# The first group's projections reordered for an early start, and 36 more filler matmuls, in a three-stage decoder layer on one core

## The chip, the cores and the metric

The kernel runs on one core of a Trainium2 chip. The time is the device time of one execution in microseconds; the median of three runs of the kernel before is 1218.7 (1215.97 to 1222.55). The profiled execution took 1217.05, of which 1215.3 lie between its first and its last instruction (the span).

## The reference, cut to what matters

x is 16 sequences of 128 rows of 256 numbers, float32. Three stages follow each other, each on a layer norm of what the one before left:

```python
def mamba(h):                                # x = x + mamba(norm(x))
    hs, gate = split(h @ in_proj.T)          # 512 channels each
    u = silu(conv4(hs) + conv_b)             # 4 taps along the sequence
    dt, B, C = split(u @ x_proj.T)           # 64, 16, 16; each rms-normed
    dt = softplus(dt @ dt_proj.T + dt_b)
    h_t = exp(dt * A) * h_(t-1) + dt * u * B # 512 channels x 16 states
    y = (sum_n h_t * C + u * D) * silu(gate)
    return y @ out_proj.T
def mlstm(q, ctx):                           # x = x + mlstm(norm(x), ctx)
    ...                                      # 4 heads of 64, gated causal scores,
    ...                                      # row norm, a norm for each head
def nodes(x):                                # x = x + norm(nodes(norm(x)))
    for c in range(6):                       # a graph of 6 attention nodes
        q, k, v = (ew * (node[..] @ We[..] + be[..]) for each of the three)
        node[c] = act_w[c] * (softmax(q@Wq (k@Wk).T / sqrt(32)) v@Wv) @ Wo[c] + q
```

## The kernel before, in words

The 16 sequences are worked in 8 groups (NG) of two, so that a tile has 256 columns (T). For a group the kernel has three streams of steps: "a" (the mamba stage's projections, 11 steps), "u" (its state sums, 16 units, each a product on VectorE at L1068, "feed", a recurrence along the sequence at L1075, "scan", a product with C at L1084, "weigh", and four matmuls into the bank MY at L539 that fold the states, "add"), "x" (the mlstm stage) and "f" (the six nodes). Four units make a chunk, whose dt and dt*u (dts, dtus) are spread over the partitions by DMA; the first chunk of the first group goes directly (`first_chunk`), the others by way of DRAM. The ring has three buffers: a feed waits until the add three units before it is done.

The order in which each engine issues the steps is written out: every step has a number (A_AT, U_AT, X_AT, P_AT, W_AT, plus a shift for each group), all steps of all groups are sorted by it into ORDER, and each engine walks that list and issues its part (`walk`). An engine works its instructions in that order and waits with semaphores (`after`). While the nodes of group g run on TensorE, the mamba and mlstm stages of group g+1 run beside them; only the first group has nothing beside it. So there is a start-up of two parts: the head (from the launch to the first feed), and the stretch from the first state sums to the first node.

Into the start-up also falls the preparation of the node weights ("prep", three parts for each of six nodes). TensorE multiplies the edge weights into the query, key and value weights (12 matmuls at L465) and the edge biases by the weights (12 matmuls with one column at L473, four at L453), ScalarE reads the products (L755), VectorE scales the rest (L981, L982) and the biases (L986, L988, L993). SyncE loads the next node's eight weight tiles of 256 KB (L358) once the last part has let the staging tiles go (w_used).

Warm steps ("w", L479) are matmuls of 128x256 on constants into the bank FA, whose product nobody reads: 10 before the walk and 24 in it. The profile counts a float32 matmul as two passes.

The head of the first group, in the order of its chain: LayerNorm of x (VectorE, L1001 to L1009), transposes (TensorE, L484), four products with win in the bank MA, each waiting until ScalarE has read the one before (L506; L774 and L779 read the first two, L785 and L788 the gates), the convolution (VectorE, L1031, six operations for each half of the channels), Silu (L788 to L792), x_proj (L515), the rms norm (L797 to L802, L1040, whose result is xdn), dt_proj (L528), the softplus (L811 to L827, L1046, L1051), and the DMAs of the first chunk.

## Time and profile before

| What | Value |
|---|---|
| median of three runs | 1218.7 us |
| profiled execution | 1217.05 us, span 1215.3 us |
| TensorE busy | 1086.6 us (89% of the span) |
| VectorE busy | 980.1 us (81%) |
| ScalarE busy | 733.2 us (60%) |
| mean granted TensorE clock | 0.95 of full speed |
| DMA | 76.06 MB, 63 GB/s over the span |

Busy times count each engine alone and overlap each other. The clock is the one that the chip granted TensorE, as a share of 2.4 GHz: 1.00 is that level, 0.50 is 1.2 GHz. A row of a timeline gives the start and length of a run of like instructions; the brackets at its end give how long the engine stood idle before it and what ended the wait.

### The profile page before, as it was taken

Reading aid. Unit: us, or ns where it says so; the run is one execution under the profiler, and the core shown is the slowest. Engines: PE = TensorE matmul, PEld = TensorE weight load, DVE = VectorE, ACT = ScalarE, POOL = GpSimd, SP = SyncE. Lnnn points to the kernel's source line nnn. Section 1 sums busy time; section 2 is a strip of 40 time slices with the busy share of each in tenths; the row PEclk is TensorE's granted clock in tenths of the full one; section 3 lists DMA queues with packets and bytes.
Section 4 is the critical chain, followed back from the end, with each engine's and each line's share of the span. In section 5 each row is a group of like instructions: output and inputs, shape, how many; then the busy total and the mean of one; then the engine's idle time right before and its main releaser. Section 6 shows DMA issues by size and latency. Waiting matters only on the chain.

```text
span 1215.3 us, 26865 instructions
## 1 busy us (share of the span) xinstructions
PE 1086.6 (89%) x11428; PEld 836.1 (69%) x11428; DVE 980.1 (81%) x1220; ACT 733.2 (60%) x1728; POOL 15.2 (1%) x33
## 2 busy tenths in 40 slices
PE   8866679999999998999899989999999988998886
PEld 6743466767777676767676767677776766776675
DVE  3398979799998999999999989999898989735222
ACT  3535442776577666776587657765686656554443
POOL 4000000000000000000000000000000000000000
PEclk9777686999999999999999999999999999999999
DMA  6721433104110412041112201041104110000000
GB/s 204 221 101 47 153 115 121 36 18 124 45 62 11 132 36 70 8 135 37 36 37 84 87 16 61 19 124 45 53 7 136 36 62 2 2 1 10 2 1 10
DMA packets 48694, 76.06 MB, mean 63 GB/s; under 512 B 5504, under 2 KB 33408, under 8 KB 48576
## 3 DMA queue, kind: packets, MB, share of 16 engines
q1 hardware_dynamic: 47872, 73.81, 19.0%
q8 instruction: 89, 1.46, 0.5%
q0 software_dynamic: 704, 0.56, 0.2%
q14 instruction: 29, 0.24, 0.1%
HBM read 62.55 MB, written 10.75 MB: 60 GB/s over the span
## 4 chain that ended last, share of the span: by engine, by line
PE 57%; DVE 15%; ACT 7%; issue 5%; DVEq 0%; ACTq 0%
PE ps L634 7%; PE heads L644 6%; PE ps L712 6%; PE heads L665 4%; PE ps L615 4%; PE ps L705 4%; PE ps L539 4%; PE heads L673 3%; DVE ring L1075 3%; DVE mx L1178 3%; PE ps L506 3%; PE ps L562 2%; PE heads L615 1%; PE ps L690 1%; ACT qT L901 1%
## 5 line engine op out<-in xcount | busy, mean ns | idle before, releaser
L1075 DVE TENSOR_TENSOR_SCAN ring<-dec,ring 128x1024 f32<-128x1024 f32 x128 | 292.3, 2283 | 1.4 <-ACT dec L846 1.1
L846 ACT ACTIVATE dec<-dts,a_neg 128x254 f32<-128x254 f32 x512 | 220.0, 500 | 19.9 <-DVE ring L1075 17.6
L1178 DVE TENSOR_REDUCE mx<-heads 128x16 f32<-128x2048 f32 x48 | 109.8, 2288 | 62.5 <-PE heads L665 61.9
L1084 DVE TENSOR_TENSOR ring<-ring,cs 128x1024 f32<-128x1024 f32 x128 | 156.2, 1220 | 1.9
L1068 DVE TENSOR_TENSOR ring<-dtus,bs 128x1024 f32<-128x1024 f32 x128 | 155.3, 1219 | 2.1 <-PE ps L539 1.5
L921 ACT ACTIVATE pr<-heads 128x512 f32<-128x512 f32 x192 | 99.1, 602 | 38.8 <-PE heads L678 38.8
L539 PE MATMUL ps<-ring,fold 128*32 128x256 f32 x1024 | 87.1, 411 | 26.4 <-DVE ring L1084 26.1
L712 PE MATMUL ps<-aT,wo_f 128*128 128x256 f32 x384 | 95.0, 388 | 11.3 <-DVE aT L1187 11.0
L634 PE MATMUL ps<-node,wq_f 128*128 128x256 f32 x384 | 94.9, 390 | 3.4 <-ACT node L936 3.4
L705 PE MATMUL ps<-node,we_f 128*128 128x256 f32 x384 | 95.1, 391 | 0.0
L644 PE MATMUL heads<-wv_f,node 128*128 128x256 f32 x384 | 93.3, 386 | 0.0
L712 PEld LDWEIGHTS ps<-aT,wo_f 128*128 128x128 f32 x384 | 69.4, 190 | 30.4 <-DVE aT L1187 21.6
L634 PEld LDWEIGHTS ps<-node,wq_f 128*128 128x128 f32 x384 | 69.7, 190 | 27.3 <-ACT node L936 18.6
L644 PEld LDWEIGHTS heads<-wv_f,node 128*128 128x128 f32 x384 | 70.9, 190 | 14.9 <-issue 6.2
L615 PE MATMUL ps<-node,wk_f 128*128 128x256 f32 x320 | 79.8, 392 | 0.0
L705 PEld LDWEIGHTS ps<-node,we_f 128*128 128x128 f32 x384 | 71.5, 194 | 11.0 <-issue 0.6
L901 ACT ACTIVATE qT<-ps,fb 128x256 f32<-128x256 f32 x96 | 40.3, 471 | 56.3 <-PE ps L634 55.3
L506 PE MATMUL ps<-th,win 128*128 128x256 f32 x256 | 66.0, 403 | 8.0 <-ACT u L779 5.8
L665 PE MATMUL heads<-kT,qT 32*128 32x128 f32 x1536 | 56.3, 282 | 17.5 <-ACT qT L901 12.8
L665 PEld LDWEIGHTS heads<-kT,qT 32*128 32x128 f32 x1536 | 48.2, 186 | 31.9 <-issue 31.9
L615 PEld LDWEIGHTS ps<-node,wk_f 128*128 128x128 f32 x320 | 57.5, 189 | 17.1 <-issue 8.6
L936 ACT ACTIVATE node<-ps,fb 128x256 f32<-128x256 f32 x96 | 40.2, 469 | 44.2 <-PE ps L712 44.2
(185 smaller groups left out, 1748.5 us busy)
## 6 DMA issues: line engine op xcount, KB each, us to landing
dts<-dt_rows SPq DMA_DIRECT2D x31, 512.0 KB, 3.9
dtus<-dt_rows SPq DMA_DIRECT2D x31, 512.0 KB, 5.3
node<-in_w_edgeT SPq DMA_DIRECT2D x18, 256.0 KB, 3.6
bs<-bc_rows SPq DMA_DIRECT2D x32, 128.0 KB, 5.0
cs<-bc_rows SPq DMA_DIRECT2D x32, 128.0 KB, 5.1
dt_rows<-dt SPq DMA_DIRECT2D x32, 128.0 KB, 2.4
dt_rows<-th SPq DMA_DIRECT2D x32, 128.0 KB, 2.5
xin<-in_x SPq DMA_DIRECT2D x8, 256.0 KB, 3.4
```

The lines of the kernel that those rows point to most:

```text
L539: last = mm(MY[SD * blk:SD * (blk + 1), 0:T], fold[:], ring[(i * UNITS + k) % RING][:, blk, :], start=(q == 0), stop=(q == NGRP - 1), tile ...
L615: last = mm(bank[:, a * T:(a + 1) * T], w[:, k, a * P:(a + 1) * P], src[:, k, :], start=(k == 0), stop=(k == HC - 1))
L634: last = mm(FA[:, a * T:(a + 1) * T], wq_f[c][:, k, a * P:(a + 1) * P], src[:, k, :], start=(a == 0 and k == 0), stop=(k == HC - 1), skip_ ...
L644: last = mm(X3[:, b * H:(b + 1) * H], node[SLOT[GRAPH[c]["v"]]][:, k, b * L:(b + 1) * L], wv_f[c][:, k, :], start=(k == 0), stop=(k == HC ...
L665: last = mm(heads[:, h, to], qT[at], kT[c % 2][at], start=True, stop=True, tile_position=(FD * h, 0))
L705: mm(ED[:, a * T:(a + 1) * T], we_f[c][:, k, a * P:(a + 1) * P], src[:, k, :], start=(a == 0 and k == 0), stop=False, skip_group_check=True)
L712: last = mm(ED[:, a * T:(a + 1) * T], wo_f[c][:, k, a * P:(a + 1) * P], aT[:, k, :], start=False, stop=(k == HC - 1), skip_group_check=True)
L846: last = fn(dec[k % 2][:, blk, :, 1:L], dts[c % 2][:, blk, :].rearrange("p (b t) -> p b t", b=GB)[:, :, 1:L], ACT.Exp, scale=a_neg[:, c, b ...
L1068: v.tensor_tensor(ring[(i * UNITS + k) % RING][:], dtus[c % 2][:], bs[:, q:q + 1, :].broadcast_to([P, BLKS, T]), ALU.mult).then_inc(sig["i ...
L1075: v.tensor_tensor_scan(states, dec[k % 2][:].rearrange("p k b t -> p (k b t)"), states, 0.0, ALU.mult, ALU.add).then_inc(sig["state"], 1)
L1084: v.tensor_tensor(states[:], states[:], cs[:, q:q + 1, :].broadcast_to([P, BLKS, T]), ALU.mult).then_inc(sig["outflow"], 1)
L1178: v.tensor_reduce(mx[:].rearrange("p (h s) -> p h s", h=HPC)[:, :, 0:STEPS], heads[:].rearrange("p h (s k) -> p h s k", s=STEPS), AX.X, AL ...
```

## The change: a new order of the head, other banks, and 36 more matmuls

The first group's streams "a" and "x" get tables of their own (A0_AT, X0_AT), the preparation and the warm steps new ones (P_AT, W_AT). The preparation of node 0 moves from the middle of the first group's projections to behind dt_proj, and that of node 1 from the head into the state sums; so do its weight loads. The third product with win goes to the bank MY and the second to ED, so that the first three need not wait for a reader. The Silu of u is done in two halves, each on the half of the convolution that is done; both gates are read with Silu directly; x_proj takes its second half when the second Silu is done. The decay constants (a_neg) are made before the rms norm. The softplus of chunk 0 starts before the second part of dt is read. SyncE issues one of the eight spreads of B and C ahead of the first chunk and seven behind it. VectorE takes the statistics of x before it makes its constants. The warm steps are 60 and not 24; from the eleventh on they multiply by win (weights) and not by the tile of zeros, and the last seven wait until VectorE has copied the last head's values (h_read). The names of the steps and what they compute stay.

```diff
-P_AT = [-416, -414, -412, -362, -312, -205, -86, -81, -67, -46, -36, -32, -25, -19, -16, -5, -3, -1]
+P_AT = [-590, -588, -107.5, -86.25, -80.5, -80, -64, -61.25, -57.75, -46, -33.75, -32.25, -23.5, -20.25,
+        -19.25, -7.25, -2.25, -0.25]
...
+A0_AT = [-1281.25, -1281.25, -1278.25, -1243, -1242.5, -1242.5, -1242.5, -1226.5, -1209.25, -593.75, -588]
+X0_AT = [-102.25, -32, -31.5, -25.25, -22.5, -21.5, -21.25, -18.25, -17, -14.5, -11.75, -11.75, -10.75, -9.25,
+         -7, -2.25]
...
     ORDER += [(FSLOTS * (g - 1) + at + _shift[g], 1 + _rank, g, n, step)
-              for g in range(NG) for n, (step, at) in enumerate(zip(_steps if g or _name != "x" else X0_STEPS, _at))]
+              for g in range(0 if _name == "u" else 1, NG) for n, (step, at) in enumerate(zip(_steps, _at))]
+ORDER += [(at, 1, 0, n, step) for n, (step, at) in enumerate(zip(A_STEPS, A0_AT))]
+ORDER += [(at, 3, 0, n, step) for n, (step, at) in enumerate(zip(X0_STEPS, X0_AT))]
...
+WARM_ZERO = 10
+WARM_HEADS = 53
+W_STEPS = [("w", "warm", n) for n in range(60)]
...
+        -22, -10.75, -10.75, -10.75, -10.75, -10.75, -10.75, -10.75]
 ORDER += [(at, 5, 0, n, step) for n, (step, at) in enumerate(zip(W_STEPS, W_AT))]
 ORDER = [(step, g) for _, _, g, _, step in sorted(ORDER)]
...
+        IN_BANK = ((MA, ED, MY, MA), (MA,) * 4)
...
                     if i == 0:
-                        for q in range(NGRP):
-                            spread_rows(0, q)
+                        spread_row(0, 0, 0)
...
                         sp.wait_ge(sig["dt_c0"], 1)
                         first_chunk(sp, dts, dt, "dt")
+                        for q in range(NGRP):
+                            for j in range(1 if q == 0 else 0, 2):
+                                spread_row(0, q, j)
...
             def warm(_, n):
-                mm(FA[:, 0:T], ones[:], zeros[:], start=True, stop=True)
+                if n == WARM_HEADS:
+                    after(pe, "h_read", 0, XH)
+                mm(FA[:, 0:T], ones[:], zeros[:] if n < WARM_ZERO else win[:, 0, 0:T], start=True, stop=True)
...
                         after(pe, "xnT_ready", i, 1)
-                    else:
+                    elif i:
                         after(pe, "inproj_read", i, j)
+                    elif j == 3:
+                        after(pe, "inproj_read", 0, 1)
...
-                            last = mm(MA[:, a * T:(a + 1) * T], win[:, k, m * P:(m + 1) * P], xnT[:, k, :],
+                            last = mm(IN_BANK[i > 0][j][:, a * T:(a + 1) * T], win[:, k, m * P:(m + 1) * P], xnT[:, k, :],
...
                 if step == 7:
                     if i == 0:
                         pe.wait_ge(sig["wx_loaded"], 16 * 2)
                     after(pe, "inproj_read", i, 4)
-                    after(pe, "u_ready", i, 1)
+                    if i == 0:
+                        pe.wait_ge(sig["u_first"], 1)
+                    else:
+                        after(pe, "u_ready", i, 1)
                     for k in range(IC):
+                        if i == 0 and k == 2:
+                            after(pe, "u_ready", i, 1)
                         last = mm(MA[:, 0:T], wx[:, k, :], u[i % 2][:, k, :], start=(k == 0), stop=(k == IC - 1))
                     last.then_inc(sig["xproj_ps"], 1)
...
+                if i == 0 and step == 4:
+                    act.wait_ge(sig["conv_first"], 1)
+                    fn(u[0][:, 0:2, :], u[0][:, 0:2, :], ACT.Silu).then_inc(sig["u_first"], 1)
+                    after(act, "inproj_ps", 0, 3)
+                    fn(gate[0][:, 0:2, :].rearrange("p a b -> p (a b)"), MY[:], ACT.Silu).then_inc(sig["inproj_read"], 1)
+                if i == 0 and step == 5:
+                    after(act, "inproj_ps", 0, 4)
+                    gates = fn(gate[0][:, 2:4, :].rearrange("p a b -> p (a b)"), MA[:], ACT.Silu)
+                    gates.then_inc(sig["inproj_read"], 1)
+                    after(act, "conv_done", 0, 1)
+                    fn(u[0][:, 2:4, :], u[0][:, 2:4, :], ACT.Silu).then_inc(sig["u_ready"], 1)
+                    act.preload_act_table_set("natural_log_exp_and_others")
+                    after(act, "inproj_read", 0, 4)
+                    act.sem_inc(sig["gate_ready"], 1)
...
                 if step == 7:
+                    if i == 0:
+                        act.wait_ge(sig["alog_loaded"], 16 * IC * BLKS)
+                        fn(a_neg[:], a_neg[:], ACT.Exp).then_inc(sig["setup_act"], 1)
+                        act.wait_ge(sig["setup_act"], 1)
+                        fn(a_neg[:], a_neg[:], ACT.Copy, scale=-1.0).then_inc(sig["setup_act"], 1)
                     after(act, "xproj_ps", i, 1)
                     after(act, "u_ready", i, 1)
                     fn(xsq, MA[:, 0:T], ACT.Square).then_inc(sig["xsq"], 1)
...
-                        if i == 0 and c == 1:
-                            act.wait_ge(sig["dt_read"], 1)
+                        if i == 0 and c == 0:
+                            last.then_inc(sig["c0_tail"], 1)
...
-            act.wait_ge(sig["vec_consts"], 1)
             act.preload_act_table_set("natural_log_exp_and_others")
             act.wait_ge(sig["vec_consts"], 2)
...
                 for b in range(GB):
                     last = v.bn_aggr(mean_var[:, b, :], stats[:, b, :])
                 last.then_inc(sig[f"ln_var{n}"], 1)
+                if i == 0 and n == 1:
+                    setup()
                 after(dve, f"ln_rstd{n}", i, 1)
...
                     if step == 4:
                         ins.then_inc(sig["conv_done"], 1)
+                    elif i == 0:
+                        ins.then_inc(sig["conv_first"], 1)
```

On ScalarE, in the head: "th<-ps" is the copy of the transposed rows or the start of the rms norm, "u" the convolution's channels, "wq_f" to "wv_f" the node weights. Before:

```order
L785 ACTIVATE gate<-ps 128x512
L755 ACTIVATE wq_f<-heads,vec 128x512
L755 ACTIVATE wk_f<-heads,vec 128x512
L755 ACTIVATE wv_f<-heads,vec 128x512
L788 ACT_TABLE_LOAD
L788 ACTIVATE gate<-ps 128x512
L790 ACTIVATE gate<-gate 128x512
L792 ACTIVATE u<-u 128x1024
L793 ACT_TABLE_LOAD
L797 ACTIVATE th<-ps 128x256
L801 ACTIVATE th<-ps 128x256
L802 ACTIVATE th<-th 128x256
```

and after:

```order
L809 ACT_TABLE_LOAD
L809 ACTIVATE u<-u 128x512
L811 ACTIVATE gate<-ps 128x512
L814 ACTIVATE gate<-ps 128x512
L817 ACTIVATE u<-u 128x512
L818 ACT_TABLE_LOAD
L836 ACTIVATE a_neg<-a_neg 128x64
L838 ACTIVATE a_neg<-a_neg 128x64
L841 ACTIVATE th<-ps 128x256
L845 ACTIVATE th<-ps 128x256
L846 ACTIVATE th<-th 128x256
L855 ACTIVATE dt<-ps,vec 128x256
```

The three reads of node weights are gone from between the projections and the Silu, two table loads stand on either side of the Silus, and the two operations on a_neg stand ahead of the first operation of the rms norm.

On TensorE, in the head: "ps<-zeros,ones" are the warm steps, "ps<-th,win" the products with win, "heads<-node", "heads<-qT,node", "heads<-kT,node" and the ones with vec the preparation of a node. Before:

```order
L479 MATMUL ps<-zeros,ones 128x256 x15
L484 MATMUL ps<-cst,th 128x128 x4
L506 MATMUL ps<-th,win 128x256 x12
L465 MATMUL heads<-node 128x256 x4
L465 MATMUL heads<-qT,node 128x256 x4
L465 MATMUL heads<-kT,node 128x256 x4
L473 MATMUL heads<-vec,node 128x1 x4
L473 MATMUL heads<-vec,qT 128x1 x4
L473 MATMUL heads<-vec,kT 128x1 x4
L506 MATMUL ps<-th,win 128x256 x4
L453 MATMUL heads<-fb,aT 128x1 x4
```

and after:

```order
L497 MATMUL ps<-zeros,ones 128x256 x10
L502 MATMUL ps<-cst,th 128x128 x4
L526 MATMUL ps<-th,win 128x256 x16
L540 MATMUL ps<-u,wx 128x256 x4
L544 MATMUL ps<-th,cst 128x256
L497 MATMUL ps<-zeros,ones 128x256 x3
L553 MATMUL ps<-xdn,wdt 128x256 x4
L481 MATMUL heads<-node 128x256 x4
L481 MATMUL heads<-qT,node 128x256 x4
L481 MATMUL heads<-kT,node 128x256 x4
L489 MATMUL heads<-vec,node 128x1 x4
L489 MATMUL heads<-vec,qT 128x1 x4
```

Five warm steps are gone ahead of the transposes, the preparation that stood between the third and the fourth product stands behind dt_proj ("ps<-xdn,wdt"), and three warm steps stand ahead of dt_proj where there was one.

On TensorE, ahead of the first node: "ps<-vaug,ml_buf" are the last head's values, "ps<-cst,hrow" the transposes whose result the first node takes. Before:

```order
L602 MATMUL ps<-vaug,ml_buf 128x65 x4
L465 MATMUL heads<-node 128x256 x4
L465 MATMUL heads<-qT,node 128x256 x4
L465 MATMUL heads<-kT,node 128x256 x4
L473 MATMUL heads<-vec,node 128x1 x4
L473 MATMUL heads<-vec,qT 128x1 x4
L473 MATMUL heads<-vec,kT 128x1 x4
L539 MATMUL ps<-ring,fold 32x256 x4
L484 MATMUL ps<-cst,hrow 128x128 x4
```

and after:

```order
L627 MATMUL ps<-vaug,ml_buf 128x65 x4
L497 MATMUL ps<-win,ones 128x256 x7
L481 MATMUL heads<-node 128x256 x4
L481 MATMUL heads<-qT,node 128x256 x4
L481 MATMUL heads<-kT,node 128x256 x4
L489 MATMUL heads<-vec,node 128x1 x4
L489 MATMUL heads<-vec,qT 128x1 x4
L489 MATMUL heads<-vec,kT 128x1 x4
L564 MATMUL ps<-ring,fold 32x256 x4
L502 MATMUL ps<-cst,hrow 128x128 x4
L469 MATMUL heads<-fb,aT 128x1 x4
```

The seven warm steps with the wait for h_read stand between the last head and the preparation of node 5; the rest keeps its order.

From the first node on all engines issue the same instructions in the same order as before.

## Rows read from the trace of the kernel before

**Rows 1.** Windows: busy us and count per engine, granted TensorE clock, DMA share, GB/s.
```profile
57.00:212.30 155.30, 115.99 (x571) 82.60 (x570) 137.24 (x174) 66.68 (x152) 0.00 (x0) 0.71 0.33 112
212.30:1215.30 1003.00, 923.25 (x10658) 714.24 (x10654) 825.78 (x1001) 641.55 (x1531) 0.00 (x0) 0.99 0.15 47
```

**Rows 2.** Waits of VectorE, 57 to 212.3 us: total us, times, longest.
```profile
DVE u L1031 <- ACT u L779: 3.9, 2, 3.0
DVE ml_buf L1114 <- ACT ml_buf L869: 2.7, 1, 2.7
```

**Rows 3.** Timeline, TensorE, start-up: start, length, line, tiles, count, idle before.
```profile
1.25 9.74 PE L479 MATMUL ps<-zeros,ones 128*128 128x256 f32 x30 [1.25 <-POOL zeros L1225]
10.82 0.60 PE L484 MATMUL ps<-cst,th 128*128 128x128 f32 x4
...
33.36 2.50 PE L515 MATMUL ps<-u,wx 128*128 128x256 f32 x8 [1.46 <-ACT u L792]
...
38.99 1.13 PE L528 MATMUL ps<-xdn,wdt 128*128 128x256 f32 x4 [0.69 <-DVE xdn L1040]
...
42.67 2.99 PE L465 MATMUL heads<-node 128*128 128x256 f32 x8
45.50 1.89 PE L465 MATMUL heads<-qT,node 128*128 128x256 f32 x8
```

**Rows 4.** Timeline, ScalarE, start-up and first table switch behind it.
```profile
32.17 1.05 ACT L792 ACTIVATE u<-u 128x1024 f32<-128x1024 f32 x1
...
35.90 0.38 ACT L797 ACTIVATE th<-ps 128x256 f32<-128x256 f32 x1 [1.38 <-PE ps L515]
...
52.44 3.29 ACT L846 ACTIVATE dec<-dts,a_neg 128x254 f32<-128x254 f32 x8 [2.17 <-DMA dts<-dt]
...
111.22 1.28 ACT L793 ACT_TABLE_LOAD   x1
112.52 2.49 ACT L846 ACTIVATE dec<-dts,a_neg 128x254 f32<-128x254 f32 x6
```

**Rows 5.** Timeline, VectorE, start-up and the first state sums.
```profile
15.80 2.46 DVE L1031 SCALAR_TENSOR_TENSOR u<-hs_pad,vec,u 128x256 f32<-128x256 f32 x6 [7.21 <-ACT u L779]
...
38.46 0.48 DVE L1040 SCALAR_TENSOR_TENSOR xdn<-ps,vec,th 128x256 f32<-128x256 f32 x1 [6.29 <-ACT th L802]
...
48.28 0.48 DVE L981 TENSOR_SCALAR we_f<-node,vec 128x512 f32<-128x512 f32 x1
...
51.72 0.47 DVE L986 TENSOR_SCALAR fb<-heads,vec 128x2 f32<-128x2 f32 x3 [2.57 <-PE heads L473]
...
54.59 2.36 DVE L1068 TENSOR_TENSOR ring<-dtus,bs 128x1024 f32<-128x1024 f32 x2 [0.21 <-DVE fb L993]
56.87 2.28 DVE L1075 TENSOR_TENSOR_SCAN ring<-dec,ring 128x1024 f32<-128x1024 f32 x1
...
67.45 1.22 DVE L1068 TENSOR_TENSOR ring<-dtus,bs 128x1024 f32<-128x1024 f32 x1
```

**Rows 6.** Timeline, VectorE, the first group's last head values.
```profile
197.68 0.47 DVE L1136 COPY hrow<-ps 128x130 f32<-128x130 f32 x2
```

**Rows 7.** Timeline, TensorE, from the state sums to the first node.
```profile
53.98 9.83 PE L479 MATMUL ps<-zeros,ones 128*128 128x256 f32 x34
...
153.55 5.66 PE L562 MATMUL ps<-wout,gate 128*128 128x256 f32 x16
...
206.12 1.03 PE L473 MATMUL heads<-vec,kT 128*128 128x1 f32 x8
...
212.30 2.93 PE L615 MATMUL heads<-node,wk_f 128*128 128x256 f32 x6
```

**Rows 8.** Windows of TensorE alone: busy, granted clock, DMA share, GB/s.
```profile
52.00:58.00 6.00, 5.75 (x18) 0.50 0.84 235
58.00:64.00 6.00, 6.00 (x33) 0.95 0.97 341
182.00:200.00 18.00, 16.37 (x62) 0.50 0.57 194
```

43 lines of the change are left out of this document (19 added, 24 removed), and 3 rows, old and new, of the table W_AT.

## Prediction

> **What bounds the kernel now.** I began with the windows, cut at the first state sum (57 us) and at the first node (212.3) [rows 1]. Behind 212.3 TensorE is busy 923 of 1003 us at a granted clock of 0.99, and the change leaves every engine's order there as it is, so I take these 1003 us as they are. Between 57 and 212.3 VectorE is busy 137.24 of 155.3 us while TensorE's clock is 0.71: VectorE sets this stretch, TensorE only where VectorE waits for it. Ahead of 57 nothing is full. There I read the timelines of the three engines, which show one chain that passes from engine to engine. So the first question is when the first feed starts, the second what the stretch from there to the first node gains or loses.
>
> **The head.** I go down the chain with the start times of before, and put the new ones beside them.
>
> Warm steps. Five fewer stand ahead of the transposes. The 30 passes took 9.74 us, 0.325 on average, but a block of eight passes in this chain takes 1.89 when the clock is high [rows 3], 0.22 each with its tail left out. The ten that go are the last ones: 2.2 us (3.2 by the mean). The transposes, at 10.82 before, start at 8.6, if the normalised rows are there. VectorE's statistics now run ahead of its constants, so that they should be.
>
> Projections to xdn. The first convolution starts 15.80 - 10.82 = 5.0 us behind the transposes [rows 3, 5], that is at 13.6. The first three products have a bank each and run back to back, so the second half is there in time, and both halves take 2 x 2.46 = 4.9: 18.5. The Silu of the second half (half of the 1.05 of before [rows 4], with its start-up 0.6) ends at 19.1. Before, the Silu ended at 33.22. The preparation of node 0, which stood between, is gone from here. Then ScalarE loads its other table, 1.28, and makes a_neg, 0.5: 20.9. x_proj's second half (half of 2.50 [rows 3]) is over by then. From the first operation of the rms norm to the start of xdn it was 38.46 - 35.90 = 2.56 [rows 4, 5]: xdn starts at 23.5 and not 38.46, 15.0 us earlier.
>
> The table load is now on the chain, and the first one stands close to it. In the trace the operation behind a load starts at 112.52, 1.30 us after the load began at 111.22 [rows 4], so I charge 1.28. The Trainium skill ("ScalarE: Activation LUTs", What ACT_TABLE_LOAD costs) puts a switch at about 2.66 us, the load and a drain of 1.38. By that page the head would be 1.4 us later, or 2.8 if the first load counts too. The trace has no such drain, and the sum goes by the trace.
>
> dt_proj to the first feed. Three warm steps now stand ahead of dt_proj, six passes: 1.3 us at the fast pace, 2.6 at the slow one, beside the 2 us in which ScalarE and VectorE finish xdn. I let dt_proj start at 24.0 (before 38.99), 23.9 to 25.2. Its second half waits for dt_read, which now comes behind the softplus of chunk 0 (three operations more on ScalarE, 1.35 us), so the preparation of node 0 starts 42.67 - 38.99 + 1.3 = 5.0 us behind dt_proj, at 29.0. A preparation takes 51.72 - 42.67 = 9.05 us until VectorE has its biases [rows 3, 5]: 38.1. Behind it stand fb (0.47) and a small one; L993 no longer stands ahead of the feed. So the first feed starts at 38.6 and the first scan 56.87 - 54.59 = 2.3 later, at 40.9. Before it was 56.87: **16.0 us earlier**.
>
> What could be late instead is the transfer. From xdn to the landing of the first chunk it was 52.4 - 38.46 = 13.9 us, with eight spreads ahead of it in SyncE's queue [rows 4, 5]. Even unimproved that is 37.4, ahead of 38.6; with seven of the eight moved behind it, earlier. If it went as before to the end of ScalarE's first four decays, the loss would be under 1 us. For the head I keep 14.5 to 17.5.
>
> **From the first scan to the first node.** This was 155.4 us (56.87 to 212.3).
>
> One more preparation (node 1) and the last piece of node 0 fall into this stretch: two operations of 0.48 and fb of 0.47 [rows 5], three small ones of about 0.2 each: 1.9 us of VectorE. The work of node 1's matmuls itself is beside it, in TensorE's 155.3 - 116.0 = 39 idle us [rows 1], but node 2's now stands ahead of an add: 0.8, with 0 to 3 as its ends.
>
> Twenty warm steps, 40 passes, stand between node 0's preparation and the first add. 34 passes took 9.83 us, the first six us at a clock of 0.50, the rest at 0.95 [rows 7, 8]. Forty take 9.83 + 6 x 0.22 = 11.2. They start 1.9 us behind the first feed, at about 39.6 (behind the four matmuls of L453), and end at 50.8, and the add at 51.4. The feed that needs it, the fourth, stood at 67.45 [rows 5], now 67.45 - 16.0 = 51.4. So it costs 0 to 1, I take 0.4; at a clock that never rises it would cost 6.
>
> The out-projection took 5.66 us for 16 passes at a clock near 0.5 [rows 7], 3.6 at full clock, which the warm steps ahead of it could give. The mlstm gates behind it make VectorE wait 2.7 us [rows 2], and the new order puts feeds and a scan there. Against that VectorE now waits for the out-projection. I take -2.4; the ends are 0 and -3.9, the latter if the whole 1.2 us of the biases' matmuls and a part of the gates' wait come on top. The largest wait, 3.9 us for the convolution of group 1 [rows 2], has no warm step ahead of it, and I leave it.
>
> The seven warm steps ahead of node 5's preparation wait for h_read, whose copies ended at 198.15 [rows 6]. Before, the preparation had begun ahead of that and ended at 207.15 [rows 7]; it now begins 3.1 us (14 passes fast) to 6.1 (slow) behind it and takes 8.1 at a high clock: 11.2 to 14.2 behind h_read where it was 9.0. The transposes behind it needed hrow 10.1 us behind h_read anyway. Loss 1.1 to 4.1, less up to 1.7 if the first node's keys (eight passes, six of them recorded as 2.93 us [rows 7]) then run at the fast pace. I take +1.6.
>
> The sum of this stretch is +1.9 + 0.8 + 0.4 - 2.4 + 1.6 = **+2.3**, with -2 and +9 as its ends.
>
> **The sum.** 1217.05 - 16.0 + 2.3 = 1203.3 for an execution like the profiled one. The median of the runs shown is 1.65 above it, so a measured time lies between 1203.3 and 1205: I say **1204**.
>
> **The rivals.**
>
> A, the fillers pay more than I gave them. VectorE stands idle 155.3 - 137.24 = 18.06 us in the stretch [rows 1], and through its last part the clock is 0.50 from 182 to 200 us [rows 8]. If the warm steps raise the clock for the group-1 projections, the heads and the first keys, half of that idle time goes: -9 where I have -2.4, so 1204 - 6.6 = about 1197. For it: between 52 and 64 us the same instructions brought the clock from 0.50 to 0.95 [rows 8]. Against: most fillers stand alone in a unit of 4.6 us. The Trainium skill ("TensorE: Matmul & The Clock Gate", What's actually happening) says that the low clock is the default and activity releases it; rows 8 agree for a solid block, and no row shows it for scattered ones.
>
> B, the fillers come in the way. The first add is late by up to 6, the seven ahead of node 5 cost 4.1 and node 2's preparation 3 of VectorE's time: 1204 + 7 = about 1211. For it: 0.50 from 182 to 200 us, where a filler pass costs twice as much.
>
> C, slower than before. One mechanism: all 36 added matmuls lie on the path at the slow pace. A pass then takes 0.43 (2.50 us for eight passes, two of them quicker, bounds it from below at 0.31 [rows 3]), so 72 passes are 31 us, and the time is 1203 + 31 - 1 (what I already count) = 1233. It decides against the change from 15 us on the path, that is from half of them. Against it: VectorE is busy 137 of 155 us [rows 1] and cannot be made to wait for most of them.
>
> D, the change doesn't do what it says: the chain is shorter but the first scan waits for a transfer. The DMAs were at 0.84 to 0.97 of their capacity from 52 to 64 us [rows 8]; if the first chunk lands where it did, at 52.4, the scan starts at 55 and the time is 1217. Against: the loads of node 1's weights, which ran there, come later now.
>
> **How the numbers follow.** My forecast 0.50, A 0.21, B 0.22, C 0.03, D 0.04. The likeliest case gives 1204. The range takes in A and B with their spread, 1194 to 1212; C, D and the ends of A and B lie outside. About 0.5% (6.1 us, 1212.6) is what a measurement of this kernel can tell from no change. Faster by more: the forecast, A, and most of B, 0.92. Within it: the rest of B and D, 0.05. Slower: C, 0.03.
>
> **What would show it.** Right: the transposes start near 8.6, xdn near 23.5, the first feed near 38.6 ended by the biases of node 0 and not by a DMA; the fourth feed waits under 1 us for the first add; the first node's keys start near 198.6 (212.3 - 13.7); and 1003 us follow. Wrong: a table load with more than 1.3 us around it; a first feed released by a DMA; VectorE idle more than 18 us between the first scan and the keys, with TensorE on warm steps as what it waits for; or another length of the part from the first node on.

## The result, and the profile after the change

The changed kernel took 1210.14 us (median of 6 runs, 1210.02 to 1212.64), the kernel before 1218.7 beside it (6 runs, 1215.97 to 1222.55). The ratio is 0.9935, its 95% interval 0.9916 to 0.9954: faster, by 0.46 to 0.84%. I had forecast 1204, in a range of 1194 to 1212.

The profiled execution took 1212.64 us, with a span of 1210.8 (before 1215.3). It is the slowest of the six, 2.5 us above their median, while the profiled one of the kernel before lies 1.65 below its median; so the two profiles lie 4.5 us apart and the two medians 8.6. In the profile the head came out as forecast, and the rest did not:

| | before | after | difference | forecast |
|---|---|---|---|---|
| first transposes start | 10.82 | 8.32 | -2.5 | 8.6 |
| first convolution | 15.80 | 13.30 | -2.5 | 13.6 |
| xdn | 38.46 | 22.58 | -15.9 | 23.5 |
| first feed | 54.59 | 37.71 | -16.9 | 38.6 |
| first scan | 56.87 | 39.98 | -16.9 | 40.9 |
| first node's keys | 212.30 | 200.69 | -11.6 | 198.6 |
| end of the span | 1215.3 | 1210.8 | -4.5 | -13.7 |
| length, first scan to keys | 155.4 | 160.7 | +5.3 | +2.3 |
| length, keys to end | 1003.0 | 1010.1 | +7.1 | 0 |

So, between these two profiles, 16.9 us were won ahead of the first scan, and 12.4 were given back behind it: 5.3 up to the first node and 7.1 behind it, in a part whose instructions stand in the same order in both kernels.

**The head.** TensorE's timeline, first 28 us (start, length, line, tiles, count, idle before and its releaser), against [rows 3]:

```profile
1.25 7.24 PE L497 MATMUL ps<-zeros,ones 128*128 128x256 f32 x20 [1.25 <-POOL zeros L1268]
8.32 0.60 PE L502 MATMUL ps<-cst,th 128*128 128x128 f32 x4
9.70 7.14 PE L526 MATMUL ps<-th,win 128*128 128x256 f32 x32 [0.78 <-ACT th L793]
...
23.12 1.13 PE L553 MATMUL ps<-xdn,wdt 128*128 128x256 f32 x4
26.59 1.57 PE L553 MATMUL ps<-xdn,wdt 128*128 128x256 f32 x4 [2.33 <-ACT dt L855]
27.95 3.18 PE L481 MATMUL heads<-node 128*128 128x256 f32 x8
```

All four products run as one block of 32 passes, in which no wait is recorded. Ahead of the preparation TensorE stands 2.33 us behind the softplus, and the clock is low when it begins: its first eight passes take 3.18 us, while the next two blocks of eight take 1.89 each. ScalarE's rows have the two table loads close together:

```profile
15.01 1.28 ACT L809 ACT_TABLE_LOAD   x1
16.30 0.63 ACT L809 ACTIVATE u<-u 128x512 f32<-128x512 f32 x1
...
18.82 1.28 ACT L818 ACT_TABLE_LOAD   x1
20.11 0.26 ACT L836 ACTIVATE a_neg<-a_neg 128x64 f32<-128x64 f32 x1
...
20.56 0.36 ACT L841 ACTIVATE th<-ps 128x256 f32<-128x256 f32 x1
```

And VectorE's, against [rows 5]:

```profile
22.58 0.48 DVE L1085 SCALAR_TENSOR_TENSOR xdn<-ps,vec,th 128x256 f32<-128x256 f32 x1 [4.44 <-ACT th L846]
...
37.19 0.47 DVE L1027 TENSOR_SCALAR fb<-heads,vec 128x2 f32<-128x2 f32 x3 [3.55 <-PE heads L489]
...
37.71 2.35 DVE L1113 TENSOR_TENSOR ring<-dtus,bs 128x1024 f32<-128x1024 f32 x2
39.98 2.29 DVE L1120 TENSOR_TENSOR_SCAN ring<-dec,ring 128x1024 f32<-128x1024 f32 x1
```

The wait ahead of the first feed is for the biases of node 0 (L489), not for a transfer.

**The two stretches behind it**, as windows (start:end, length, then busy us and count of TensorE, its weight loads, VectorE, ScalarE and GpSimd, the granted clock, DMA share, GB/s), against [rows 1], and VectorE's largest waits in the first of them, against [rows 2]:

```profile
40.00:200.70 160.70, 136.14 (x711) 101.19 (x709) 139.35 (x183) 68.71 (x155) 0.00 (x0) 0.82 0.39 127
200.70:1210.80 1010.10, 931.93 (x10658) 720.44 (x10654) 826.41 (x1001) 641.54 (x1531) 0.00 (x0) 0.98 0.15 46
```

```profile
DVE fb L1034 <- PE heads L469: 2.8, 3, 1.1
DVE u L1137 <- PE ps L564: 2.8, 1, 2.8
DVE fb L1027 <- PE heads L489: 2.4, 3, 1.3
DVE u L1074 <- ACT u L804: 2.1, 1, 2.1
```

Three things are to be seen. VectorE's work in the first stretch grew by 2.1 us (137.24 to 139.35), as forecast. Its idle time grew too, from 18.06 to 21.35, although the granted clock rose from 0.71 to 0.82: the old waits shrank (the convolution's from 3.9 to 2.1), and new ones for TensorE's head preparations (L469, L489) and for an add stand in their place. And behind the keys the same 10,658 matmuls are busy 931.93 us instead of 923.25, at 0.98 instead of 0.99.

**Where the 7.1 us are.** I marked node 5's query block of each group and node 0's of the next in TensorE's timeline. From the first to the last query block of a group both kernels take the same time to 0.2 us (107.2 in most groups). All the rest lies at the seven boundaries, from node 5's block of one group to node 0's of the next, and in the tail behind the last block:

| start to start, us | 0/1 | 1/2 | 2/3 | 3/4 | 4/5 | 5/6 | 6/7 | tail | first query block to end |
|---|---|---|---|---|---|---|---|---|---|
| before | 21.84 | 21.84 | 21.84 | 22.89 | 24.47 | 22.11 | 20.63 | 21.38 | 999.6 |
| after | 23.42 | 22.98 | 22.96 | 22.89 | 24.56 | 22.11 | 21.76 | 22.98 | 1006.5 |

The same boundary is either 21.84 or about 1.1, 1.6 or 2.7 longer. Here is 0/1 in TensorE's timeline, of the kernel before, where it is short:

```profile
329.50 0.66 PE L602 MATMUL ps<-vaug,ml_buf 128*128 128x65 f32 x4 [1.36 <-DVE ml_buf L1130]
...
340.39 0.66 PE L484 MATMUL ps<-cst,hrow 128*128 128x128 f32 x4 [1.36 <-DVE hrow L1009]
...
341.82 0.63 PE L484 MATMUL ps<-cst,th 128*128 128x128 f32 x4 [0.34 <-ACT node L895]
...
342.95 1.99 PE L615 MATMUL heads<-node,wk_f 128*128 128x256 f32 x8
```

and of the kernel after, where it is long, with the clock in windows of 1 us under it:

```profile
318.22 0.66 PE L627 MATMUL ps<-vaug,ml_buf 128*128 128x65 f32 x4 [1.36 <-DVE ml_buf L1175]
...
329.11 0.66 PE L502 MATMUL ps<-cst,hrow 128*128 128x128 f32 x4 [1.36 <-DVE hrow L1052]
...
330.54 0.75 PE L502 MATMUL ps<-cst,th 128*128 128x128 f32 x4 [0.34 <-ACT node L936]
331.22 1.08 PE L564 MATMUL ps<-ring,fold 128*32 128x256 f32 x8
332.23 3.01 PE L640 MATMUL heads<-node,wk_f 128*128 128x256 f32 x8
```

```profile
331.00:332.00 1.00, 1.00 (x10) 0.20 (x8) 0.93 (x5) 0.20 (x1) 0.00 (x0) 0.50 0.00 0
...
333.00:334.00 1.00, 1.00 (x4) 0.82 (x3) 1.00 (x3) 0.49 (x2) 0.00 (x0) 0.50 0.03 8
334.00:335.00 1.00, 1.00 (x5) 0.83 (x5) 1.00 (x2) 0.00 (x0) 0.00 (x0) 0.84 0.46 146
```

The waits are the same to 0.01 us (1.36, 1.36, 0.34). Behind the last of them the clock falls to 0.50 in the one execution and not in the other, for 3.4 us, and the keys' block takes 3.01 instead of 1.99. Such falls, counted by the excess over the shortest value of each boundary in any run: four before, nine after (at 4/5 of the kernel after two of them follow each other without a break, 6.8 us at 0.50). Their sum is 4.9 us before and 11.6 after, which makes 6.7 of the 7.1 us.

Where a fall begins is regular in a way that the waits are not. In the kernel after, the falls of 1/2 to 4/5 begin at 450.4, 580.1, 709.8 and 839.5 us, 129.7 apart each time, while the query blocks ahead of them start 130.4, 130.1 and 130.1 apart:

```profile
450.40:453.80 3.40, 3.40 (x34) 2.72 (x31) 3.19 (x8) 2.06 (x4) 0.00 (x0) 0.50 0.30 77
580.10:583.50 3.40, 3.40 (x51) 3.00 (x51) 3.13 (x10) 1.34 (x4) 0.00 (x0) 0.50 0.28 80
709.80:713.20 3.40, 3.40 (x53) 2.93 (x52) 2.78 (x9) 0.63 (x2) 0.00 (x0) 0.50 0.28 77
```

In every profile of this case the changes of the clock keep to such a beat: the moments at which the clock changes lie whole multiples of one and the same step apart, to 0.01 us, and where they lie in the program differs from one execution to the next. Continued from one fall, they mark the whole trace. Of the 77 boundaries in the eleven profiles whose gap ahead of the last head's values isn't filled, the 50 in which a moment of the beat comes 6.6 to 8.3 us behind node 5's query block have a fall there, and the other 27 have none. The wait of 1.36 us ends 6.6 us behind the start of that block. So the same wait brings a fall or not by where it lies against the beat.

### The profile page after: what moved, and what is told of

It reads as the page before. It is cut to its first block, busy times and chain, and to the rows that moved or that the text cites. A ratio compares the mean times of both kernels' runs of the same rounds, so it can differ in the third digit from the quotient of the medians.

```text
span 1210.8 us, 27037 instructions
## 1 busy us (share of the span) xinstructions
PE 1100.8 (91%) x11500; PEld 848.7 (70%) x11500; DVE 980.5 (81%) x1220; ACT 732.6 (61%) x1728; POOL 15.2 (1%) x33
## 4 chain that ended last, share of the span: by engine, by line
PE 60%; DVE 13%; ACT 7%; issue 5%; DVEq 0%; ACTq 0%
PE ps L659 7%; PE heads L669 6%; PE ps L737 6%; PE ps L730 5%; PE heads L690 4%; PE ps L640 4%; PE heads L698 4%; PE ps L564 4%; DVE ring L1120 3%; DVE mx L1223 3%; PE ps L526 3%; PE ps L587 2%; PE heads L640 1%; PE ps L715 1%; PE ps L599 1%
## 5 line engine op out<-in xcount | busy, mean ns | idle before, releaser
L730 PE MATMUL ps<-node,we_f 128*128 128x256 f32 x384 | 100.0, 406 | 0.0
L564 PE MATMUL ps<-ring,fold 128*32 128x256 f32 x1024 | 86.4, 406 | 12.6 <-DVE ring L1129 12.2
L730 PEld LDWEIGHTS ps<-node,we_f 128*128 128x128 f32 x384 | 75.2, 204 | 12.6 <-issue 1.4
```

The lines of the kernel that those rows point to most:

```text
L564: last = mm(MY[SD * blk:SD * (blk + 1), 0:T], fold[:], ring[(i * UNITS + k) % RING][:, blk, :], start=(q == 0), stop=(q == NGRP - 1), tile ...
L730: mm(ED[:, a * T:(a + 1) * T], we_f[c][:, k, a * P:(a + 1) * P], src[:, k, :], start=(a == 0 and k == 0), stop=False, skip_group_check=True)
```

## The experiments

"Fillers" are matmuls on constants, two passes each, whose result nobody reads. The step of a group whose output product is node 5's is the anchor for them in the order. One such pass takes 0.22 to 0.26 us at the high clock (six take 1.46 or 1.56), not the 0.11 that an expectation below gives. Ratios are against the kernel before, run beside each on the same chip, with their 95% intervals. The experiments come in three sets, each on a chip of its own, and times compare best within one set.

### First set: fillers at the boundary, the 36 steps, the early warm steps

**after_fill and before_fill**: three fillers in TensorE's 1.36 us gap between node 5's output product and the transposes behind it, in each kernel.

```diff
+FILLS = 3
+ORDER += [(FSLOTS * g + F_STEPS.index(("f", "node", NODES - 1)), 0.5, g, n, ("w", "fill", n))
+          for g in range(NG - 1) for n in range(FILLS)]
...
+            def fill(_, n):
+                mm(FA[:, 0:T], ones[:], win[:, 0, 0:T], start=True, stop=True)
...
```

> The changed kernel with three more matmuls of 128x256 on constants (weights and ones, bank FA) between the out-projection of node 5 and the transposes that follow, in each of the first seven groups, where TensorE stood idle 1.36 us. Theory 1 (clock at the group boundaries): the part behind the first node is not the same in both kernels because at a boundary the granted clock may fall to 0.50, by chance of when the boundary comes, at about 1.1 us each (1.57 for the first); the fillers keep it up, and the lead at the first node (11.3 us) is kept to the end: about 1204 us, no group boundary with a step in the lead. Theory 2 (the loss behind the first node is one of order: some engine starts the nodes with more left to do): the fillers fit in idle time or cost up to 1.3 us a boundary, so 1210 to 1219 us, and the lead shrinks as before.

> The kernel before with the same three fillers at the same seven places. Theory 1: before had three boundaries with a fallen clock, so it gains about 3 us: about 1215.5, and the distance to the changed kernel with the fillers is 11 us and not 8.6. Theory 2: 1218 to 1228, and the distance stays at 8.6.

Measured: after_fill 1207.14 (ratio 0.9904, 0.9868 to 0.9940), before_fill 1215.18 (0.9987, 0.9961 to 1.0013). They lie 8.0 us apart: the 11 us of theory 1 did not come, since both kernels keep falls elsewhere. In the profiles the long values of 23.4 and 24.5 are gone, and values about 1.1 us above the shortest are left at four boundaries of seven in after_fill and at three in before_fill. So there are two places where the clock falls, and these fillers close one. The other lies in node 5, 12 to 16 us ahead of the next group's queries, behind the other gap of 1.36 us. The timeline of TensorE in after_fill5 (below), at a boundary of 22.88, shows it (the block of 32 passes at its end takes 1.17 us at the high clock), and the windows beside it:

```profile
572.83 0.71 PE L631 MATMUL ps<-ml_buf,ctxT 64*128 64x128 f32 x4
574.90 0.88 PE L638 MATMUL ps<-vaug,ml_buf 128*128 128x65 f32 x4 [1.36 <-DVE ml_buf L1186]
...
575.92 2.09 PE L709 MATMUL heads<-qT,kT 32*128 32x128 f32 x32
```

```profile
575.00:576.00 1.00, 1.00 (x9) 0.78 (x9) 0.19 (x1) 0.00 (x0) 0.00 (x0) 0.60 0.00 0
576.00:577.00 1.00, 1.00 (x20) 1.00 (x24) 0.83 (x6) 0.28 (x1) 0.00 (x0) 0.50 0.00 0
```

**after_no36**: the kernel after without its last 36 warm steps; the other 24 stay.

```diff
-ORDER += [(at, 5, 0, n, step) for n, (step, at) in enumerate(zip(W_STEPS, W_AT))]
+ORDER += [(at, 5, 0, n, step) for n, (step, at) in enumerate(zip(W_STEPS[:24], W_AT[:24]))]
```

> The changed kernel without its last 36 warm steps (the ones from the state sums to the first node); the 24 ahead stay. Theory F0 (the fillers do little: their delays pay for their clock): the first node's keys start at 199 to 202 us where they start at 200.7 now. Theory F+ (they are worth what the forecast's rival A says): keys at 205 or later. Theory F- (they stand in the way, as VectorE's 2.8 us wait for the last add behind them shows): keys at 197 or 198. Behind the keys the time depends on the clock at the boundaries, 1003 to 1010 us, by theory 1.

Measured: 1212.45 (0.9951, 0.9926 to 0.9976), 2.3 us above the 1210.14 of the kernel after, with intervals that overlap. Its profile has the first scan at 39.45 and the keys at 201.54: a stretch of 162.1 where the kernel after has 160.7. That is what theory F0 said of the keys. Taking the 36 out doesn't shorten the stretch, so they are not what made it longer than before.

**after_late4**: four more warm steps ahead of the first transposes (14, one fewer than before the change).

```diff
-WARM_FIRST = 10
+WARM_FIRST = 14
```

> The changed kernel with four more warm steps ahead of the first transposes, whose only direct cost is a later start of everything: 8 passes at 0.22, 1.7 us. Theory 1: the lead over the kernel before goes through other steps, since the boundaries come at other moments of the clock; the part from the first query block to the end differs from the changed kernel's by 1 us or more in one direction. Theory 2: the same instructions in the same order take the same time, so everything is 1.7 us later from the transposes to the end, and the part behind the first node does not change by more than 0.3.

Measured: 1213.6 (0.9954, 0.9923 to 0.9985). The transposes start at 9.37 (after: 8.32) and xdn at 23.64 (22.58), 1.05 later each. But the first scan starts at 39.70, 0.28 earlier than in the kernel after. The preparation of node 0 begins with

```profile
28.60 1.89 PE L481 MATMUL heads<-node 128*128 128x256 f32 x8
```

at the high clock, where the kernel after has 3.18 for this block. So in this pair of profiles what the dropped warm steps gave at the front, the low clock took back before the first scan. From the first query block to the end it takes 1007.1 us against 1006.5: 0.6, between the 1 us of theory 1 and the 0.3 of theory 2. Its falls stand at other boundaries, as theory 1 says (2/3 takes 24.49 where the kernel after has 22.96, 4/5 22.95 where that has 24.56).

### Second set: the second gap, and node 0's preparation

**after_fill5 and before_fill5**: as above, and two fillers more, in another bank, ahead of node 5's output product (the wait of 1.12 us).

```diff
+ORDER += [(FSLOTS * g + F_STEPS.index(("f", "node", NODES - 1)), -0.5, g, n, ("w", "fillx", n))
+          for g in range(NG - 1) for n in range(2)]
...
```

> The changed kernel with five fillers at each of seven group boundaries: two matmuls of 128x256 on constants into a free bank ahead of node 5's out-projection, where TensorE waits 1.1 us for the attention rows, and three behind it (as in after_fill, which still showed a fallen clock at two of its boundaries). Theory 1: no boundary falls any more, the lead over the kernel before at the first node (11.3 to 12.1) is kept or grows by the dips that the kernel before has, and the spread of its times shrinks: median 1202 to 1205. Theory 2 (the clock falls at a boundary whatever TensorE does there): 1207 or more, with dips left.

> The kernel before with the same five fillers at the same places. Theory 1: median 1213 to 1215, and the distance to after_fill5 is that of the two kernels at the first node, 10 to 12 us, where the two kernels without fillers lie 8.6 apart. Theory 2: the distance is under 8.

Measured: after_fill5 1207.8 (0.9921, 0.9894 to 0.9949), before_fill5 1216.64 (1.0000, 0.9978 to 1.0022). The boundaries are those of after_fill and before_fill to 0.05 us: this gap has no part in it. Theory 1 was a miss in both: after_fill5 is not at 1202 to 1205 and keeps its falls, and the two lie 8.8 us apart, not 10 to 12. It left the gap ahead of the last head's values as the candidate.

**after_no36_fill5**: both edits together.

> The changed kernel with the five fillers at the boundaries and without the 36 warm steps between the state sums and the first node. If the 36 do nothing (as the equal start of the first node in after_no36 says: lead at its query block 11.5 against 11.45), the time is that of after_fill5 within 1.5 us. If they are worth something by the state in which they leave the clock: 3 us or more slower.

Measured: 1211.07 (0.9949, 0.9928 to 0.9971), 3.3 us above after_fill5; its keys start at 203.70, after_fill5's at 199.07, and behind the first query block both take the same time (1002.0 and 1002.2).

**after_prepmid**: the first two parts of node 0's preparation back between the third and the fourth product, nothing else.

```diff
-P_AT = [-590, -588, -107.5, ...
+P_AT = [-1242.4, -1242.2, -107.5, ...
-A0_AT = [-1281.25, -1281.25, -1278.25, -1243, -1242.5, -1242.5, -1242.5, -1226.5, ...
+A0_AT = [-1281.25, -1281.25, -1278.25, -1243, -1242.5, -1242.3, -1242.3, -1226.5, ...
```

> The changed kernel with the preparation of node 0 put back between the third and the fourth product with win (parts 1 and 2 of three; the last stays where the change put it); banks, halves of the Silu and all else as changed. Theory P (moving the preparation off the chain is the largest part of the head's gain): the first xdn comes at 31 to 34 us and not 22.6, the first feed then waits for the chunk's transfer, and the first scan starts at 45 to 48 and not 40.0. Rival (the preparation is on the path wherever it stands, since the first feed waited for its biases in the changed kernel): the first scan within 2 us of 40.

Measured, one run: 1218.65. xdn at 35.22 (after: 22.58), first feed 46.96, first scan 49.24, keys 209.40. The move of the preparation alone is worth 12.6 us at xdn and 9.3 at the first scan. Theory P held, and its sizes were too small; the first feed waits 0.62 us for the chunk's transfer, as it said. Part of the price in the old place is another transfer (and part are slow passes: x_proj takes 3.62 us where after_late4 has 1.98):

```profile
17.33 1.99 PE L481 MATMUL heads<-node 128*128 128x256 f32 x8 [2.74 <-DMA aT<-in_w_node]
```

### Third set: all gaps of the boundary filled, and one bank

**after_fillall, before_fillall**: as the five fillers, and three more (five in the last group) in the gap of node 5 between the last scores and the last head's values.

```diff
+_max5 = F_STEPS.index(("f", "max", NODES - 1))
+ORDER += [(FSLOTS * g + _max5, 3, g + 1, 11.5 + n / 100, ("w", "fill", n)) for g in range(NG - 1) for n in range(3)]
+ORDER += [(FSLOTS * (NG - 1) + _max5 + 0.5, 2.5, NG - 1, n, ("w", "fill", n)) for n in range(5)]
```

> The kernel after with short matmuls on constants (0.11 us each at full clock) at three places of every group: two ahead of node 5's output product, three ahead of the next group's node 0, and three more (five in the last group) in node 5 between the last scores and the last head's values, where TensorE idles 1.36 us (2.40 in the last group). Theory F (every interval between node 5's query block and the next node 0's of 22.9 us is a clean one of 21.8 plus one fall of the clock): all seven intervals come to 21.84 (the sixth about 21.0, the seventh 20.6), first query block to end about 995 to 999 us (after 1006.5), median 1201 to 1205. Rival N (the second fall is set by something else, and the matmuls only take room): intervals of 22.9 remain in the same numbers as with five fillers, 1207 to 1209.

> The same matmuls in the kernel before. Theory F: its intervals come to 21.84 as well, first query block to end falls from 999.4 to 995 to 997, median 1212 to 1214, so the difference to the changed kernel with the same matmuls is the head's alone, 10 to 12 us. Rival N: as the kernel before, 1216 to 1218.

| start to start, us | 0/1 | 1/2 | 2/3 | 3/4 | 4/5 | 5/6 | 6/7 | tail | first query block to end |
|---|---|---|---|---|---|---|---|---|---|
| after_fill5 | 21.83 | 21.84 | 22.88 | 21.83 | 22.90 | 22.01 | 21.70 | 24.26 | 1002.2 |
| before_fill5 | 21.82 | 21.83 | 21.84 | 22.90 | 22.88 | 20.97 | 21.74 | 22.94 | 999.4 |
| after_fillall | 21.85 | 21.85 | 21.86 | 21.84 | 21.84 | 20.98 | 20.62 | 21.31 | 995.1 |
| before_fillall | 21.85 | 21.84 | 21.86 | 21.85 | 21.84 | 20.98 | 20.62 | 21.34 | 996.2 |

Measured: after_fillall 1203.56 (6 runs, 1199.93 to 1206.9; ratio 0.9874, 0.9853 to 0.9896), before_fillall 1214.02 (0.9962, 0.9947 to 0.9977). Theory F held. Every boundary is at its shortest, in both, and no fall is left at one (inside a group one is: the seventh of before_fillall takes 98.5 us between its query blocks, where all others take 97.0). TensorE's timeline of after_fillall at 0/1 shows the gap filled, with the rows behind it at full pace (the last head's values 323.88 - 322.45 = 1.43 us behind the first filler, where 1.36 us of waiting stood):

```profile
322.45 1.56 PE L508 MATMUL ps<-win,ones 128*128 128x256 f32 x6
323.88 0.66 PE L641 MATMUL ps<-vaug,ml_buf 128*128 128x65 f32 x4
...
337.34 1.99 PE L654 MATMUL heads<-node,wk_f 128*128 128x256 f32 x8
```

The interval of after_fillall lies wholly below that of the kernel after (0.9916 to 0.9954): it beats both kernels. Against before_fillall it is 10.5 us faster (the ratios, 0.0088 of 1218.6, say 10.7). That is what the change itself is worth when the boundaries are clean in both; the kernels as they stood showed 8.6. The profile of after_fillall, with its late keys, is of the slowest of its six executions.

**after_no36_fillall**: the same without the last 36 warm steps.

> As the first of this call but without the 36 matmul pairs between the first state sum and the first node (the first 24 pairs stay). It values the 36 alone, with no falls of the clock at the group boundaries to blur it. If the 36 are worth what the medians so far say (1212.45 against 1210.14, 1211.07 against 1207.8): 2 to 4 us slower than the first of this call, its first keys 2 to 4.6 us later. If they are worth nothing: within 1 us.

Measured: 1203.18 (4 runs, 1202.55 to 1203.91; 0.9880, 0.9861 to 0.9899), the same as after_fillall, with 36 steps fewer: either is the version to keep. With the 2.3 and 3.3 us of the other two pairs, the 36 steps are worth between nothing and some 3 us, and the runs don't settle where. The two profiles are of one kernel, but for the 36, and their keys start at 206.30 and 203.36: the one with the fillers is the later. Up to the keys after_fillall has the instructions of after_fill5, whose keys start at 199.07. The difference is again the clock. This is TensorE ahead of the out-projection in after_fillall:

```profile
137.12 2.93 PE L505 MATMUL ps<-win,ones 128*128 128x256 f32 x6
...
141.41 5.70 PE L601 MATMUL ps<-wout,gate 128*128 128x256 f32 x16
```

and in the kernel after:

```profile
136.67 1.56 PE L497 MATMUL ps<-win,ones 128*128 128x256 f32 x6
...
139.18 3.70 PE L587 MATMUL ps<-wout,gate 128*128 128x256 f32 x16
```

From the start of the first of these blocks to the end of the last it is 10.0 us in one execution and 6.2 in the other. VectorE of after_fillall waits there twice, for the preparation and for the out-projection's result:

```profile
141.58 0.22 DVE L1048 SCALAR_TENSOR_TENSOR fb<-heads,vec,bias_t 128x2 f32<-128x2 f32 x1 [2.80 <-PE heads L477]
...
147.20 0.23 DVE L1162 TENSOR_TENSOR wgate<-wgate 128x72 f32<-128x72 f32 x1 [2.79 <-issue]
```

The second wait is marked as issue; what it stands for is the end of the block at 141.41 + 5.70 = 147.11.

**after_onebank**: the first three products of the first group back in one bank with the fourth, each waiting until the one before has been read.

```diff
-        IN_BANK = ((MA, ED, MY, MA), (MA,) * 4)
+        IN_BANK = ((MA,) * 4, (MA,) * 4)
-                    elif i:
+                    else:
                         after(pe, "inproj_read", i, j)
-                    elif j == 3:
-                        after(pe, "inproj_read", 0, 1)
...
-                    fn(gate[0][:, 0:2, :].rearrange("p a b -> p (a b)"), MY[:], ACT.Silu).then_inc(sig["inproj_read"], 1)
+                    fn(gate[0][:, 0:2, :].rearrange("p a b -> p (a b)"), MA[:], ACT.Silu).then_inc(sig["inproj_read"], 1)
```

> The kernel after with the first group's first three products (both halves of the convolution's input, and the gate) in one accumulator bank again, each waiting until the one before has been read, as in the kernel before; all else is as in the kernel after. Theory: the waits put the convolution's and the Silu's reads between the products, and with the second half of x late by a read the rms norm's product starts 3 to 5 us later (26 to 28 us where it is 22.58), the first scan as much later (43 to 45). Rival: the reads are short and hidden behind TensorE's own slow start, xdn moves under 1 us, and the head's gain comes from the moved preparation and the dropped fillers alone.

Measured, one run: 1212.28. The transposes start at 8.74, xdn at 29.58, the first scan at 46.97: 6.6 us later at both, once the 0.42 of the transposes is taken off. The products stand apart, each behind ScalarE's read of the bank:

```profile
10.15 2.87 PE L524 MATMUL ps<-th,win 128*128 128x256 f32 x8 [0.78 <-ACT th L791]
14.68 3.57 PE L524 MATMUL ps<-th,win 128*128 128x256 f32 x8 [1.66 <-ACT u L802]
20.00 1.97 PE L524 MATMUL ps<-th,win 128*128 128x256 f32 x8 [1.75 <-ACT u L802]
```

The theory held, and its size was too small. Part of the 6.6 us is the clock and not the waits themselves: the first two blocks of eight take 2.87 and 3.57 us, the third 1.97. The keys start at 204.54, only 3.85 later than after's, and the boundaries cost 3.0 us less, so that the whole of this single run ends where the kernel after did. I take the milestones of the head from it, not its total.

## Why the prediction came out as it did

**The head was right, for the reasons given.** The forecast of -16.0 met -16.9. The banks are worth 6.6 us and the moved preparation 9.3 at the first scan, each undone alone; the halves of the Silu, the early decay constants and the order of the spreads were not undone alone. The 0.9 us that it came out early are there at xdn already (22.58 for 23.5), 0.3 of them from the transposes and 0.5 from the rms norm, whose first operation starts at 20.56, 2.02 us ahead of xdn where it was 2.56. Node 0's preparation began at 27.95 where I had 29.0, and then took 37.19 - 27.95 = 9.24 until VectorE had its biases where I had 9.05. The warm steps' 2.2 us came through at the transposes (2.5), yet after_late4 shows that they need not come through at the first scan.

**The table load was right at 1.28.** The operations behind the two loads start 1.29 us after the loads did. The Trainium skill ("ScalarE: Activation LUTs", What ACT_TABLE_LOAD costs) has a drain of 1.38 on top; with two switches in this chain that would be 2.8 us at xdn, which came 0.9 us early instead. No row shows the drain.

**The first transfer was right**: rival D fell, since the first feed waits for L489 and no DMA.

**The stretch to the first node was mis-sized, +5.3 for +2.3.** VectorE's extra work was right (2.1 for 1.9; the pieces that I listed add up to 2.0). The 40 passes ran from 39.45 to 50.68 where I had 39.6 to 50.8, although I had misread the rows behind it (of the block that starts at 53.98 only the first 4 us lie in the window at 0.50, not six). The fourth feed started at 51.38 behind an add at 50.60, as forecast, and the out-projection took 3.70 us where I had 3.6. The idle time is what I missed: it grew by 3.3 us instead of 0.4, which is nearly all of the difference. The largest new wait is 2.77 us for an add (L564) at 136.89; ahead of it stand node 3's preparation, behind which the clock has fallen, and two warm steps between the adds:

```profile
132.89 1.08 PE L564 MATMUL ps<-ring,fold 128*32 128x256 f32 x8
133.90 2.08 PE L497 MATMUL ps<-win,ones 128*128 128x256 f32 x4
135.91 0.84 PE L564 MATMUL ps<-ring,fold 128*32 128x256 f32 x8
```

I had priced node 2's preparation ahead of an add, and no other, and at nothing the waits for the biases of the preparations themselves (L469 and L489, 5.2 us in six waits, where the kernel before has 0.8). The seven warm steps ahead of node 5's preparation took 5.36 us, at the slow end of my 3.1 to 6.1, and the keys came 17.4 us behind the last head copy instead of 14.2, +3.3 for +1.6. Which of these waits makes how much of the 3 us was not tried alone. The stretch of one and the same order varied from 159.7 (after_fill5) to 167.6 us (after_fillall), that is from +4.2 to +12.1 against before: the middle of my term, +2.3, lies below all of it and its upper end, +9, was too low. My own pieces, added up, give -2.6 and +10.0 as the ends.

**The step that failed is the sentence "I take these 1003 us as they are".** Its reason was true, the order of every engine is the same there, and its conclusion was false: in the profiles the part took 7.1 us more. The same pause of 1.36 us lets it fall in one execution and not in the next. By the two fillall kernels the falls are the cause: with TensorE kept busy in these gaps, both kernels go to 995 to 996 us from the first query block on. What made nine falls of four is in part chance, and in the medians the loss is smaller. A fall comes where the beat of the clock meets the wait, and the beat lies elsewhere in each execution; so one profile of each kernel can't say how many falls a kernel has as a rule. If head and stretch are alike in the median executions, which no trace shows, the part from the keys on cost 12.4 - 4.1 - 5.3 = 3.0 us there and not 7.1. The runs with all gaps filled point the same way: the two kernels are 10.5 us apart with the falls taken out and 8.6 with them (these from another set of runs), a loss of 1.9. Whether the earlier start of the first node makes falls likelier was not shown. Against a simple rule: after_prepmid, with its keys 2.9 us earlier than before's, has 1003.8, between the two.

So the total: head -16.9, stretch +5.3, rest +7.1 make the -4.5 of the span. For an execution like the profiled one I had 1203.3, and the profiled one took 1212.64: the 9.3 us are the failed step (7.1) and 3.0 of the stretch, less 0.9 from the head. The median is 6.1 above the 1204, less than that, because the profiled execution was a slow one. Rival B had the time, 1211, for another reason: a filler in the way would have stood in the stretch, not behind the first node. Rival A got its clock (0.71 to 0.82) and not its time, because the idle time of VectorE did not shrink with it. C was far off. The pieces that I had listed for B add up to 10 us above the forecast, not 7.

## What to carry to other kernels

When a change leaves a long part of the program alone, that part is still a term of the sum, with a size of its own: before taking it as fixed, look at how often TensorE's clock falls in it and how much each fall costs, and keep the whole of that as a range (here 4 to 9 falls of 1.05 to 1.6 us). Look, too, at where a profiled execution lies among all the runs of its kernel: here one was 1.65 us below its median and the other 2.5 above, and 4.1 of the 12.4 us given back between the two profiles were no loss between the medians. Where a trace shows falls behind a short wait of TensorE on the path (here 1.36 us), passes on constants that fit into the wait are worth a trial, if a bank is free. The falls are found by the interval between two marks of a repeated pattern, which takes few values and shows a fall as the step between them. Fillers scattered over a stretch that VectorE bounds raised its mean clock and, at best, moved the end by 3 us.

## What the runs showed of the hardware

- The granted clock falls from 1.00 to 0.50, that is from 2.4 to 1.2 GHz, behind TensorE waits of 1.36 us followed by short transposes or narrow products, and at the boundaries a fall lasts 3.4 us, or 6.8 as at 4/5 of the kernel after. It costs 1.05 to 1.14 us among node 5's scores and 1.6 at the transposes ahead of the keys and in the tail of the kernel after; 6.8 us of low clock, or two falls in one boundary, cost 2.6 to 2.7 (24.56 and 24.47 against 21.84).
- Whether it falls behind one and the same wait differs between executions of equal orders (21.84 or 23.42 at 0/1). The changes of the clock keep to a beat that is fixed within an execution (129.7 us apart three times in the kernel after, where the query blocks are 130.4, 130.1 and 130.1 apart) and lies elsewhere in the next; in 77 of 77 boundaries the fall in node 5 came exactly when a moment of the beat lay 6.6 to 8.3 us behind its query block. In the three kernels with all gaps filled it fell at none of 24 places, tails included, until the last 3.2 us of the program.
- One kernel's time spreads by 10 us or more, and the mean granted clock goes with it: before_fill took 1212.4 us at 0.954 and 1223.19 at 0.942, after_late4 1207.67 at 0.965 and 1218.0 at 0.952.
- The 20 first passes took 7.24 us in the profile of after and 6.04 in that of after_onebank, at the same start of 1.25 us: how early the clock rises at the program's beginning differs by over a microsecond.
